# A graph network's counting and attention stages: additions and row work moved to GpSimd, loops written out, query loads in pairs

## The reference

```
deg  = max(count of dst, 1)                       # edge_index = (src, dst)
x1 = LN(x  + relu(segsum((x[src] + rel[type]) @ Wn, dst) * deg**-0.5 + x @ Wl))
# layer 1, on the edges and on a loop at every node, 8 heads of 16:
Q, K, V = relu(x1 @ Wq + bq)[row], relu(x1 @ Wk + bk)[col], (x1 @ Wv)[col]
att   = sum over a head of Q * K
alpha = softmax of att over the edges of a row
x2 = LN(x1 + segsum(V * alpha, row) + bias)
x3 = LN(x2 + degree-normalised sum @ W)           # layer 2
out = LN(x3 + two degree-normalised layers with relu between)
```

## Time and profile before

| | |
|---|---|
| median of three runs | 2523.57 us |
| the profiled execution, its own time | 2524.51 us |
| its span, first to last instruction | 2522.7 us |
| TensorE (PE) busy | 2167.6 us, 86% |
| VectorE (DVE) busy | 1981.2 us, 79% |
| ScalarE (ACT) busy | 1186.5 us, 47% |
| GpSimd (POOL) busy | 89.3 us, 4% |
| stage of the counting, about 34 to 456 us | PE 375.4, DVE 344.5, ACT 293.5, POOL 0 us busy |
| stage of the maxima, up to 1391 us | DVE busy throughout |
| stage of the attention, about 1391 to 2181 us | PE 669.3, DVE 725.2, ACT 604.0, POOL 12.9 us busy |

### The profile page before, as it was taken

How to read it: one execution, slowest core, us unless ns; L and a number is a source line. 1 busy time by engine, 2 the same in 40 slices (tenths; PEclk the granted TensorE clock), 3 DMA queues, 4 the chain that set the end, 5 groups by cost and what they waited for, 6 DMA issues and landing times. The chain is left out here.

```text
span 2522.7 us, 38976 instructions
## 1 busy us (share of the span) xinstructions
PE 2167.6 (86%) x12483; PEld 921.4 (37%) x12570; DVE 1981.2 (79%) x2690; ACT 1186.5 (47%) x1579; POOL 89.3 (4%) x147
## 2 busy tenths in 40 slices
PE   5888988899688888888888689898988889699998
PEld 3555555466332222222222222222222222255555
DVE  7887878333399999999999699898999989743223
ACT  4676766466511112111210587787877879300000
POOL 1000000110000000000000000000000000211000
PEclk9998999999799999999999899999999999899999
DMA  0000000266700000000000444344444434200000
GB/s 20 0 0 0 0 0 0 76 207 228 227 21 6 6 6 9 6 6 6 9 6 3 108 122 108 105 122 112 119 113 114 115 103 125 56 1 1 1 9 18
DMA packets 266004, 144.83 MB, mean 57 GB/s; under 512 B 169469, under 2 KB 260883, under 8 KB 265900
## 3 DMA queue, kind: packets, MB, share of 16 engines
q1 hardware_dynamic: 265094, 143.04, 20.3%
q10 hardware_dynamic: 806, 0.40, 0.1%
HBM read 103.43 MB, written 39.97 MB: 57 GB/s over the span
## 5 line engine op out<-in xcount | busy, mean ns | idle before, releaser
L1297 DVE CUSTOM_DVE_ANT_0 ps<-ps,max_mask 128x1536 f32<-128x1536 f32 (+1 forms) x400 | 700.7, 1864 | 14.5 <-PE ps L1251 14.5
L1550 DVE SCALAR_TENSOR_TENSOR counts<-counts,att_a 128x1792 f32<-128x1792 f32 x263 | 518.3, 2029 | 38.9 <-ACT counts L1530 38.9
L1530 ACT ACTIVATE counts<-ps 128x896 f32<-128x896 f32 x526 | 454.2, 916 | 180.9 <-PE ps L1474 179.4
L1474 PE MATMUL ps<-att_q,att_k 99*128 99x448 bf16 x1400 | 339.5, 366 | 49.6 <-issue 24.2
L1284 ACT ACTIVATE max_mask<-counts 128x3136 uint8 x24 | 67.6, 2816 | 528.6 <-DVE max_mall L1305 528.6
L480 ACT ACTIVATE counts<-ps 128x899 f32 x261 | 247.2, 947 | 135.5 <-PE ps L430 121.9
L1483 PE MATMUL ps<-counts,att_v 128*32 128x448 f32 x2104 | 260.6, 568 | 36.5 <-DVE counts L1550 8.1
L1474 PEld LDWEIGHTS ps<-att_q,att_k 99*128 99x128 bf16 x1400 | 110.4, 99 | 382.3 <-issue 169.9
L1251 PE MATMUL ps<-counts,max_q 96*128 96x512 bf16 (+1 forms) x700 | 170.0, 360 | 74.2 <-DVE max_mx L1297 52.2
L426 PE MATMUL ps<-hot 128*128 128x192 bf16 (+1 forms) x474 | 201.7, 442 | 32.3 <-DVE hot L331 32.3
L615 PE MATMUL ps<-counts 128*128 128x512 bf16 (+1 forms) x1036 | 205.7, 358 | 20.6 <-DVE counts L683 19.9
(11 more groups left out here) (209 smaller groups left out, 2471.6 us busy)
## 6 DMA issues: line engine op xcount, KB each, us to landing
att_k<-keys SPq DMA_DIRECT2D x175, 198.0 KB
att_v<-values SPq DMA_DIRECT2D x175, 128.0 KB
counts_turned<-counts SPq DMA_DIRECT2D x25, 784.0 KB, 5.0
att_a<-counts_turned SPq DMA_DIRECT2D x175, 112.0 KB
max_q<-queries SPq DMA_DIRECT2D x25, 192.0 KB, 3.0
att_q<-queries SPq DMA_DIRECT2D x7, 519.8 KB
queries<-fl_cuts SPq DMA_DIRECT2D x24, 128.0 KB
keys<-fl_cuts SPq DMA_DIRECT2D x24, 128.0 KB
```

Source lines behind the costliest of these rows:

```text
L1297: v.tensor_tensor_reduce(out=flat[:, lo:hi], in0=flat[:, lo:hi], in1=mask[slot][:, lo:hi], scale=1.0, scalar=0.0, op0=ALU.mult, op1=ALU.ma ...
L1474: last = nc.tensor.matmul(m.bank[2 * (n % NS) + z][:, 0:CW], k[i][:, 2 * h + z, :], q[:, 2 * h + z, :], start=True, stop=True)
L1530: nc.scalar.activation(e[n % NE][:, :, :], m.ps[:, 2 * (n % NS):2 * (n % NS) + 2, 0:CW], ACT.Exp).then_inc(exped, 1)
L1550: v.scalar_tensor_tensor(w, w, 1.0, a[i % DG][:, :].unsqueeze(1).to_broadcast([P, 4, CW]), op0=ALU.min, op1=ALU.mult).then_inc(weighed, 1)
```

## The change

1. Counting: the additions move from VectorE to GpSimd, with their register loads; ScalarE loads its registers every four groups instead of sixteen; the loops of TensorE, VectorE and ScalarE are written out.
2. The block behind the maxima goes. Its steps become the first steps of `attend`, with the copies shared by VectorE and ScalarE; the first chunk's queries load without the three rows, and ScalarE's queue places those rows from SBUF into the query tile. The rows for later chunks are stored by SyncE behind the loads of the third slot.
3. Queries of a chunk load by pairs of heads, in four DMAs.
4. Row work: GpSimd adds bias and residual rows, and subtracts the mean and multiplies by the root over 512 columns at once. VectorE keeps the division and the statistics, and three products of the next chunk now stand between or behind these.

```diff
+        @block.gpsimd
+        def _(pool):
...
+                    for k in range(n):
+                        pool.wait_ge(bank_free, BG * i + k + 1 + 4)
+                        pool.wait_ge(added, BG * i + k + NSH)
+                        column = m.counts[:, :, ds(base[k], 1)]
+                        pool.tensor_tensor(column, column, shared[k % NSH], op=ALU.add).then_inc(added, 1)
...
-                with pe.Fori(0, NBODY) as i:
+                for i in range(NBODY):
                     tiles(i, BG * G)
...
                     for k in range(n):
+                        if k % LOADED == 0:
+                            base = nc.values_load_multi_w_load_instructions(
+                                t.gbase[0:1, ds(BG * i + k, min(LOADED, n - k))], engines=(mybir.EngineType.Activation,),
...
             def load_queries(c, h):
+                heads = slice(2 * h, 2 * h + 2)
+                rows = KM if c else KS
+                sp.dma_start(q[0:rows, heads, :], qs[0:rows, heads, ds(c * CW, CW)]).then_inc(q_loaded[h], 16)
...
+            sp.wait_ge(neg_copied, 3)
+            for z in range(3):
+                sp.dma_start(qs[KS + z, :, :], neg[z * HEADS:(z + 1) * HEADS, :]).then_inc(neg_stored, 16)
+            sp.wait_ge(neg_stored, 48)
...
+            for c in range(NC):
+                pool.wait_ge(x_loaded, 16 * (c + 1))
+                pool.tensor_tensor(xr[:, :, :], xr[:, :, :], bb[:, :].unsqueeze(1).to_broadcast([RB, RPC, D]),
+                                   op=ALU.add).then_inc(pool_step, 1)
+                pool.wait_ge(pool_step, 2 * c + 1)
+                pool.wait_ge(weighted, 2 * c + 2)
+                pool.tensor_tensor(y[:, :, :], y[:, :, :], xr[:, :, :], op=ALU.add).then_inc(mixed, 1)
                 inverse_roots(pool, m, mv, sd, normed, rooted, c)
+                pool.tensor_tensor(y[:, :, :], y[:, :, :], wide(mv[:, :, 0]), op=ALU.subtract).then_inc(pool_step, 1)
+                pool.wait_ge(rooted, 2 * c + 2)
+                pool.wait_ge(pool_step, 2 * c + 2)
+                pool.tensor_tensor(y[:, :, :], y[:, :, :], wide(sd[:, :]), op=ALU.mult).then_inc(finished, 1)
...
+            act.wait_ge(neg_copied, 1)
+            for z in range(3):
+                act.dma_start(q[KS + z:KS + z + 1, :, :], neg[z * HEADS:(z + 1) * HEADS, 0:CW]).then_inc(neg_placed, 16)
...
                 rest(c)
                 weights(c + 1, 0)
                 take_sums(c)
                 weights(c + 1, 1, range(1))
-                rows(c)
+                weigh_rows(c)
                 weights(c + 1, 1, range(1, 2))
+                weights(c + 1, 2, range(1))
+                statistics(c)
+                weights(c + 1, 2, range(1, 2))
```

More of the change, by code:

```diff
@@ L49 @@
 NSH = 8
+LOADED = 4
 HOT = T * (WG * (SB + TB) + 2 * P)
@@ L358, in _, with rounds @@
                 one_hots(NH - 1, NH - 1).then_inc(col_ready, 1)
[L360 to L363, removed]
+                def rounds(i):
                     for q in range(BB):
                         make(BB * i + q + NH, q % NH)
[L366 to L375, removed]
+                for i in range(NBODY):
+                    rounds(i)
                 for r in range(BB * NBODY + NH, NU):
                     make(r, r % NH)
-                for g in range(left, NTG):
-                    add(g, g % NSH, base[g - left])
             with v.Else():
@@ L405, in _, with adds @@
                                   m.bank[1][:, 0:W * TB].rearrange("p (b d) -> p b d", d=W)).then_inc(any_copied, 1)
+        @block.gpsimd
+        def _(pool):
+            bad = pool.value_load(t.bad[0:1, 0:1], min_val=0, max_val=1)
+            with pool.If(bad == 0):
+                def adds(i, n):
+                    base = nc.values_load_multi_w_load_instructions(
+                        t.gbase[0:1, ds(BG * i, n)], engines=(mybir.EngineType.Pool,), min_val=0, max_val=N - 1,
+                        skip_runtime_bounds_check_because="minima of node numbers")[1]
+                    for k in range(n):
[3 more added lines that the diff above has]
+                        pool.tensor_tensor(column, column, shared[k % NSH], op=ALU.add).then_inc(added, 1)
+                for i in range(NBODY):
+                    adds(i, BG)
+                adds(NBODY, NTG - NBODY * BG)
         @block.tensor
@@ L484, in evacuate @@
                            .then_inc(bank_free, 1)
-                with act.Fori(0, NBODY) as i:
+                for i in range(NBODY):
                     evacuate(i, BG)
@@ L1323, in _, with attend @@
                     finish(SB - 1, at + SB - 1, hh, at % 2)
[L1324 to L1366, removed]
+def attend(nc, m, mall, x1, qs, ks, vd, ad, bias, out):
     with ExitStack() as ctx:
@@ L1453, in _ @@
                     load_slot(c + 1, 0, i)
[L1455 to L1458, removed]
+                for h in range(HP):
+                    hold(sp, scored, PB * (c + 1) - (HP - 1) + h, m.passed)
+                    load_queries(c + 1, h)
             load_others(NC - 1)
@@ L1516, in chunk @@
                             sums(c, d, d < 2, d >= 2 * SB - 2)
+            pe.wait_ge(neg_step, 5)
+            for b in range(SB):
+                last = nc.tensor.matmul(m.bank[b // 4][0:3 * HEADS, (b % 4) * P:(b % 4 + 1) * P],
+                                        pcs[:, b, :, :], m.identb[:, :], start=True, stop=True)
+                if b in (3, SB - 1):
+                    last.then_inc(neg_turned, 1)
+            pe.wait_ge(neg_copied, 3)
+            pe.wait_ge(neg_placed, 48)
             for c in range(NC):
@@ L1553, in rest @@
             def rest(c):
-                for i in range(2, SB):
+                for i in range(3, SB):
                     weights(c, i)
```

130 lines of the change are left out of this document (67 added, 63 removed).

## The result

The changed kernel took 2529.75 us (median of 14 runs, 2526.58 to 2530.65), the kernel before 2524.27 (14 runs): 1.0021 times as long, 95% interval 1.0013 to 1.0028. It is 5.5 us slower. The forecast was 2507, with a range up to 2523: the sign was wrong.

The account below looks back on a forecast made before the run. TensorE was taken to bound counting, VectorE's products by the counts to pace attend. Terms -34 - 12 + 28 + 1 = -17 us gave 2507 us; range 2472 to 2523, the forecast's own 2490 to 2522.

Parts of the forecast that it names:

- Counting: Counting stage: loops written out and additions off VectorE remove the waits at loop heads; 34 us off.
- end of attend: Last chunk: nothing covers the row chain, 6.3 us against 5.4 before; 1 us more.
- Start of attend: From the maxima to the first product: loads start with the stage, first product at 1403; 12 us off.
- The change of chunk: Six times in attend: later finished rows delay store, sixth tile's keys and d10; 4.7 us each, 28 us more.
- p: Price of one GpSimd operation of 512 columns in the row work: 1.1 us taken, ends 0.43 and 1.7.
- epsilon and root 1.3 (1528.23 to 1529.56) to 1531.8: Change of chunk: epsilon and root after the statistics take 1.3 us as before, ending at 1531.8.
- the free port: Rival, change of chunk: products do not hold up GpSimd's row work; 2.3 us each, total about 2493; chance 0.2.
- the harmless late store: Rival, change of chunk: the late store delays nothing and row work simply leaves VectorE; total 2454; chance 0.1.
- The dear operation: Slower rival, change of chunk: same chain with a dear GpSimd operation; at p = 3 total 2530; chance 0.05.
- starved in the counting: Slower rival: GpSimd gets its port only after a round of VectorE's three operations; 1.71 us a group, total 2565; chance 0.05.
- the three terms: Inputs of the forecast's own range: counting 22 to 36 off, start 9 to 14 off, p from 0.43 to 1.7.
- The rule cited from the Trainium skill: A two-SBUF-input VectorE instruction and a GpSimd one exclude each other entirely; gives the row chain two waits, 2.4 us in all.

Follow-up runs that it names:

- e3: Changed kernel with SyncE issuing the loads of source tiles 5 to 9 ahead of the rows' store and the next residual rows; 2469.24 us.
- e5: Changed kernel with VectorE standing still after the statistics until the finished rows are there, so GpSimd runs alone; 2490.85 us.
- e8: As e6, with three products placed between the statistics and the final scaling on VectorE; 2459.7 us.
- e6: Changed kernel with row work back on VectorE and the loads of source tiles 5 to 9 issued ahead of the store; 2467.98 us.
- e2: Changed kernel with row work back on VectorE in one piece as before, GpSimd keeping only epsilon and root; 2466.93 us.

## Why the prediction was wrong

- Counting and end of attend: right in mechanism and size (34.2 and 0.8 us for 34 and 1). The additions took 0.41 us (median), more than the 0.25 taken and more than the 0.38 at which VectorE was to lose time if it stopped for the whole of each. It did not: its round grew by 0.07 us, and it still waits for TensorE.
- Start of attend: right in size (11.8 for 12), in part by luck. The loads were to be the later stream and the negated rows to be there at 1398, 1364 on the new clock; the rows were the later ones, and the first scores, which waited for them, ran at 1366.42.
- The change of chunk: the path was right, link by link (four operations, store, keys, tile, first product; e3 shows it), and so was p: 1.04 to 1.27 us for the 1.1 taken. The step that failed is "epsilon and root 1.3 (1528.23 to 1529.56) to 1531.8". They were priced by a row in which VectorE was waiting for them; in the changed kernel it multiplies instead. Only subtraction and multiplication were given a wait for a product, but all four have one. The traces show it at each of the six changes: an operation of GpSimd that begins while a product runs ends a fixed time behind the end of that product, the 4-column addition 0.06 us, the root 0.88, the operations of 512 columns 0.90. Epsilon and root took 4.64 us (1484.09 to 1488.73) instead of 1.3, 3.3 more; e5 takes the products away and has 1.3 again. The two steps behind them came out as predicted (4.75 us for 4.7).
- Of the 3.75 us that each change cost beyond the forecast, read at the first one, the finished rows are 3.0 (1493.46; the predicted 1536.5 is 1490.5 on this clock, 45.98 earlier, the statistics having come 0.5 sooner), the loads 0.3 (4.62 us from the issue for 4.3), and a second wait after the restart 0.6 (the other changes have it in two cases of five). Six times 3.75 is 22.5, all that separates the sum from the result; 3.75 is the mean of the six. It moved SyncE's wait for the rows by 66 us, not by the 35 foreseen. TensorE waits 12.7 us for each sixth tile, not about 5; it comes to the tile at 1488.9, where the prediction's times give 1493, which costs nothing: what decides is when the tile is there.
- The rivals: the free port and the harmless late store fell. The dear operation came out near the measured time at p = 3 (2530), but its mechanism fell: alone the operation takes 1.04. What makes it long is the product beside it. GpSimd was not starved in the counting: it waits 291.3 us for ScalarE.
- The forecast's own range, 2490 to 2522, is not what its terms add up to. With all three at their slow ends (22 and 9 us off, p = 1.7) the same sum gives 2529, with all at their fast ends 2495. An edge of 2529 would have met the measured 2529.75 by luck only: none of the three terms was at its slow end.
- The rule cited from the Trainium skill ("SBUF — State Buffer", "SBUF: two separate sides") agrees with GpSimd's durations here, 1.89 for 0.20 and 2.67 for 1.01 us. It was applied to two of four instructions. On VectorE's side it holds for the operations of 512 columns (2.86 for 2.02 us) and not for the root: in e8 the root runs to 1483.27, 0.95 us into a product that still takes 2.02, so it does not keep a product out for its whole length.

That e5, with its rows in time, stays 21 us above e3 is VectorE's standing still, 21.6 us; its products take 7.9 us less than in e3, and it waits 7.7 more for scores. What stays open: the trace shows when a GpSimd operation ends, not when within its time it is let in.

## What to carry to other kernels

Work that is moved to GpSimd beside an uninterrupted row of VectorE operations is to be priced by the end of the VectorE operation it meets, as in the traces here, for every instruction of the chain, the smallest too; its duration in a place where VectorE waits for it says nothing. Before a step is made later, look what stands behind its DMA in the same queue: with the row work on GpSimd the order of the issues decided 60 us (e3), with the row work on VectorE nothing (e6 against e2), and with the loads early the sharing itself decided nothing (the intervals of e3 and e6 overlap).

## What the runs showed of the hardware

TensorE's clock fell while it waited for the sixth tile. Stretches of the first change in the changed kernel (length, busy us and instructions of PE, PEld, DVE, ACT, POOL, granted clock, DMA share, GB/s):

```profile
1480.00:1488.00 8.00, 8.00 (x60) 2.25 (x60) 7.79 (x13) 7.87 (x10) 3.83 (x2) 1.00 0.00 1
1488.00:1502.00 14.00, 0.89 (x10) 0.09 (x9) 7.35 (x3) 1.44 (x2) 6.58 (x4) 0.60 0.26 68
1502.00:1505.00 3.00, 3.00 (x12) 0.63 (x12) 0.15 (x1) 1.73 (x2) 0.00 (x0) 0.50 0.70 173
...
1508.00:1512.00 4.00, 4.00 (x30) 1.14 (x27) 3.35 (x2) 3.12 (x5) 0.00 (x0) 1.00 0.36 96
```

It restarts at 0.50, the 1.2 GHz level, with scores of 1.67 us instead of 0.93, and is back at 1.00 from 1508 on. Its first three tile halves start 3.26 and 2.94 us apart (1502.00, 1505.26, 1508.20) instead of 1.76 at full clock, and VectorE's products behind them 3.19 and 2.64: by this reading VectorE's waits of 1.17 and 0.62 us are the price of the slow clock, which no run isolates. Before, TensorE did not stop at the sixth tile, and the clock was 0.99 to 1.00 there (1536 to 1550).

A GpSimd operation of 4 columns takes 0.20 us alone and, beside products of 2.0 us, 1.04 to 1.89, by how much of the product is left when it comes; the root takes 1.02 and 2.67. A small operation does not lengthen the products (e8: 3.93 for two); one of 512 columns, 1.04 us alone, lengthens a product beside it from 2.02 to 2.86. So moving a 512-column operation of 0.69 us off VectorE costs VectorE 0.84. The 350 products of the stage take 712.8 us in e3 and 692.2 in e2, 20.6 more, and its waits for scores 5 more, where e2 has 23.6 us of additions, scaling and waiting for the root that e3 does not have.
